# One core, attention and a routed mixture of experts: weights loaded early, late tokens in memory, two shared quads moved, scatters in pairs, first rows in four loads

## What is computed

```python
x = x + tanh(g_xattn[0]) * attention(layernorm(x), ctx, ctx, masks, Wq, bq, Wk, bk, Wv, bv, Wo, bo)
h = layernorm(x)
probs = softmax(h @ router_w + router_b)
topk_p, topk_i = top_k(probs, 2);  topk_p /= sum(topk_p)
for e in range(8):
    moe += combine[e] * (gelu((h @ w1[e] + b1[e]) * gate[e]) @ w2[e] + b2[e])
shared = (gelu((h @ sw1 + sb1) * sgate) @ sw2 + sb2) * sigmoid(shared_weight)
x = x + tanh(g_ffn[0]) * layernorm(moe + shared) * (ln_g, ln_b)
```

## Time and profile before

| | |
|---|---|
| median of 3 runs | 815.27 us (813.66 to 815.3) |
| the profiled execution | 814.22 us, span 812.4 us |
| mean granted clock of PE | 0.95 |
| busy, share of the span | PE 87%, PEld 67%, DVE 76%, ACT 65%, POOL 34% |
| stages by the span | attention to 439.8, experts to 723.5, combine to the end |

### The profile page before, as it was taken

One profiled execution on the slowest core, in us unless ns is written; L12 is line 12 of the kernel. 1 busy time (PEld: TensorE's weight loads), 2 busy tenths in 40 slices (PEclk: granted clock), 3 DMA queues, 4 the chain that ended last, 5 costly groups with the idle time before them and its releaser, 6 DMA issues. The chain is left out here.

```text
span 812.4 us, 25014 instructions
## 1 busy us (share of the span) xinstructions
PE 703.1 (87%) x8074; PEld 546.8 (67%) x8075; DVE 619.3 (76%) x2328; ACT 526.3 (65%) x1117; POOL 274.6 (34%) x293
## 2 busy tenths in 40 slices
PE   2799999999999999999953799999999998967930
PEld 1466666666666666666631599999999997945620
DVE  5788988888888888888764577766666664629998
ACT  2678877878778787777520565666555664528873
POOL 5000033222333223233345146655555554520000
PEclk9999999999999999999955999999999999989975
DMA  4111121222321232311113822222222222244552
GB/s 126 40 41 48 54 81 44 70 65 76 84 81 51 61 88 73 83 42 38 38 47 132 207 67 78 75 78 68 74 69 75 73 70 62 68 114 135 171 145 87
DMA packets 74961, 64.59 MB, mean 80 GB/s; under 512 B 8320, under 2 KB 62848, under 8 KB 74624
## 3 DMA queue, kind: packets, MB, share of 16 engines
q1 hardware_dynamic: 53360, 32.96, 16.1%
q0 software_dynamic: 8448, 17.45, 6.6%
q10 hardware_dynamic: 13072, 13.12, 5.1%
HBM read 36.22 MB, written 23.09 MB: 73 GB/s over the span
## 5 line engine op out<-in xcount | busy, mean ns | idle before, releaser
L181 POOL DMA_INDIRECT expert_lists<-xn,slots x128 | 124.5, 973 | 311.9 <-PE pair L421 194.6
L1257 ACT ACTIVATE hT<-pair,b1g_c,gate_c 128x256 f32<-128x256 f32 x272 | 138.4, 562 | 101.5 <-PE pair L79 94.8
L1382 POOL DMA_INDIRECT expert_results<-y,dest x136 | 138.9, 1022 | 130.6 <-DVE y L1359 81.3
L1196 PE MATMUL pair<-w,hT 128*128 x1088 | 134.7, 277 | 0.0
L1196 PEld LDWEIGHTS pair<-w,hT 128*128 128x128 f32 x1088 | 127.0, 192 | 2.1 <-issue 0.5
L898 ACT ACTIVATE PT<-pair 128x512 f32<-128x512 f32 x128 | 75.5, 591 | 45.0 <-PE pair L434 45.0
L77 PE MATMUL pair<-rT,w_now 128*128 128x256 f32 x276 | 83.8, 303 | 4.6 <-ACT hT L1257 3.8
L577 DVE TENSOR_REDUCE mx<-pair 128x16 f32<-128x1024 f32 x64 | 78.2, 1223 | 10.0 <-PE pair L404 8.5
L1330 DVE CAST w_now<-w 128x1024 fp32r x71 | 52.7, 742 | 36.3 <-issue 36.3
L79 PE MATMUL pair<-rT,w_now 128*128 128x256 f32 x276 | 78.5, 284 | 0.0
L78 PE MATMUL pair<-rT,w_now 128*128 128x256 f32 x276 | 78.4, 284 | 0.0
(11 more groups left out here) (182 smaller groups left out, 1422.8 us busy)
## 6 DMA issues: line engine op xcount, KB each, us to landing
rows<-expert_lists SPq DMA_DIRECT2D x70, 130.0 KB
yin<-expert_results SPq DMA_DIRECT2D x16, 512.0 KB, 5.3
x_all<-in_x SPq DMA_DIRECT2D x16, 256.0 KB, 4.5
cT<-in_ctx_T SPq DMA_DIRECT2D x16, 256.0 KB
pad_k<-in_mask_BxS_ik SPq DMA_DIRECT2D x16, 256.0 KB
xn2T<-x2T ACTq DMA_DIRECT2D x16, 256.0 KB
w<-in_w ACTq DMA_DIRECT2D x4, 1024.0 KB, 15.2
out<-res ACTq DMA_DIRECT2D x7, 512.0 KB, 4.6
```

The source lines that it names most:

```text
L181: po.indirect_dma_start(lists[:, :], bass.IndirectOffsetOnAxis(ap=m.slots[:, par, t, k:k + 1], axis=0), m.xn2[:, par, t, :], None).then_in ...
L1196: last = pe.matmul(y_ps[par][:, h * D:(h + 1) * D], hT[:, par, c, h * P:(h + 1) * P], w2[:, bass.ds(e, 1), c, :].rearrange("p a d -> p (a ...
L1257: ac.activation(hT[:, par, c, :], h_ps[par][c // 2][:, (c % 2) * SL:(c % 2 + 1) * SL], ACT.Gelu, bias=b1g_c[:, c, bass.ds(e, 1)], scale=ga ...
L1382: po.indirect_dma_start(results[:, :], bass.IndirectOffsetOnAxis(ap=dest[:, par, h, :], axis=0), y[:, par, h, :], None).then_inc(sent[par] ...
```

## The change

`DRAINED = 2` quads of the shared expert go into attention's drain. Their hidden layer stands on PE behind the transposed logits of quad 14, their gelu on ACT behind the DMA of quad 15 (into `prob`), their second layer on PE ahead of the prefix sums of quad 15, and their copies at ACT's end of the block. `prepare` moves from (NQ, 1) to (NQ - 1, 1). `w2` and the first half of `w1` are loaded in attention, 256 KB with each of the last 12 quads' loads on SP. `x2T` of quads 4 to 15 goes to memory (`late_tokens`) and comes back in 12 loads of 256 KB, issued by ACT in the first 16 tiles of experts, which are now written out on ACT too. In combine the first group's rows come in four loads of 256 KB, and ACT weighs them ahead of its first gelus. Scatters are two a tile step, at all four steps; slots are ready before the weights' part of `route_b`.

```diff
     m.xn2T = sb("xn2T", [P, EARLY * QW])
+    m.w2 = sb("w2", [P, E, F // P, D])
+    m.w1a = sb("w1a", [P, E // 2, F])
...
+            def early_weights(i):
+                if i < E:
+                    sp.dma_start(m.w2[:, i], a["w2"][:, i]).then_inc(m.weights_in, 16)
+                else:
+                    sp.dma_start(m.w1a[:, i - E], a["w1"][:, i - E]).then_inc(m.weights_in, 16)
             for q in range(2, NQ):
                 load_x(q, q % 2)
                 load(q, q % 2)
                 later_load(q - 4)
+                if q >= NQ - 12:
+                    early_weights(q - (NQ - 12))
...
@@ PE, attention
+            def early_hidden(q):
+                need(pe, exped, NT - 1)
+                need(pe, max_flat, NT - 1)
+                pe.wait_ge(m.prepared, 6)
+                pe.wait_ge(x2T_kept[q], 16)
+                for c in range(SC):
+                    pe.matmul(banks[2 * q + c][:, :], m.sw1[:, c * P:(c + 1) * P], xn2T[:, q * QW:(q + 1) * QW],
+                              start=True, stop=True).then_inc(sh_done, 1)
...
                     feed_a(u, par, q)
+                    if (q, u) == (NQ, 3):
+                        for i in range(DRAINED):
+                            early_hidden(i)
+                    if (q, u) == (NQ + 1, 3):
+                        for i in range(DRAINED):
+                            early_second(i)
@@ DVE, attention
-                    if (q, u) == (NQ, 1):
+                    if (q, u) == (NQ - 1, 1):
                         prepare()
@@ ACT, attention
+                    if (q, u) == (NQ + 1, 3):
+                        need(ac, turned, NT - 1, per=2)
+                        for i in range(DRAINED):
+                            for c in range(SC):
+                                ac.wait_ge(sh_done, i * SC + c + 1)
+                                ac.activation(prob[:, i, c * QW:(c + 1) * QW], banks[2 * i + c][:, :], ACT.Gelu,
...
-                        ac.dma_start(xn2T[:, cols_of((q - 2) * QT, QT)], x2T[:, par, :]).then_inc(x2T_kept[par], 16)
+                        kept = (xn2T[:, cols_of((q - 2) * QT, QT)] if q - 2 < EARLY else
+                                tokens[:, (q - 2 - EARLY) * QW:(q - 1 - EARLY) * QW])
+                        ac.dma_start(kept, x2T[:, par, :]).then_inc(x2T_kept[par], 16)
...
+            for q in range(DRAINED):
+                ac.wait_ge(sy_done, q + 1)
+                ac.activation(xn2T[:, q * QW:(q + 1) * QW], pt_ps[q][:, :], ACT.Copy)
@@ POOL, attention
+            def scatter(n, q, first):
+                need(po, rb_step, q, per=RB_STEPS, k=3, total=NQ)
+                if q < NQ - 3:
+                    need(po, masked, n)
+                    scatter_rows(po, lists, m, q, (first,))
                     need(po, turned, n - 1, per=2)
+                    scatter_rows(po, lists, m, q, (first + 1,))
+                else:
+                    if q == NQ - 3:
+                        need(po, *((lg_done, q + 1), (lgT_done, q + 1), (pref_done, q + 1),
+                                   (xn2_ready, q + 2, QT))[first // 2], total=NQ)
+                    else:
+                        need(po, (x2T_done, lg_done, lgT_done, pref_done)[first // 2], q + 1, total=NQ)
+                    scatter_rows(po, lists, m, q, (first, first + 1))
...
+                    if u >= 2 and exists(q - 3, NQ - 1):
+                        scatter(n, q - 3, 2 * u - 4)
+                    if u < 2 and exists(q - 4, NQ - 1):
+                        scatter(n, q - 4, 2 * u + 4)
@@ ACT, experts
-            halves = [slice(k * E // 2, (k + 1) * E // 2) for k in range(2)]
-            for k, es in enumerate(halves):
-                ac.dma_start(w1[:, es, 1, :], a["w1"][:, es]).then_inc(w1_in[k], 16)
+            ac.dma_start(w1[:, E // 2:, 1, :], a["w1"][:, E // 2:]).then_inc(w1_in, 16)
             pads(ac, range(E // 2, E))
-            for es in halves:
-                ac.dma_start(w2[:, es], a["w2"][:, es]).then_inc(w2_in, 16)
...
-            iterations(ac, body)
+                if isinstance(t, int):
+                    late = NQ - EARLY
+                    for q in range(t * late // HEAD, (t + 1) * late // HEAD):
+                        ac.dma_start(m.late_T[:, q * QW:(q + 1) * QW], tokens[:, q * QW:(q + 1) * QW]).then_inc(m.late_in, 16)
+            iterations(ac, body, HEAD // 2)
@@ combine
-            for g in range(NGR):
+            for i in range(2):
+                for k in range(2):
+                    at = i * H * P + k * TOK
+                    sp.dma_start(yin[:, 0, k, i * H:(i + 1) * H], results[at:at + H * P, :]
+                                 .rearrange("(t p) d -> p t d", p=P)).then_inc(first_in[i][k], 16)
+            for g in range(1, NGR):
                 load(g)
...
+            weigh(0)
             gelu(EARLY)
             gelu(EARLY + 1)
-            weigh(0)
             weigh(1)
```

123 lines of the change are left out of this document (66 added, 57 removed).

## The result

The changed kernel takes 825.12 us (median of 4 runs, 821.45 to 826.34), the kernel before 814.75 beside it: a ratio of 1.0112 (95% interval 1.0094 to 1.0131). It is **1.1% slower**; 808.5 was forecast, and faster. The profiled execution took 821.45 us with a span of 819.6, against 814.22 and 812.4.

A forecast was written before the change was run, and what follows sets the result against it. PE was taken to bound attention and experts, so edits pay only in attention's drain and the starts of experts and combine. -6.6 - 0.8 + 1.25 = -6.15 gives 808.1 on 814.22, set at 808.5; range 803.5 to 813.0.

The forecast's parts named there:

- At nothing: Attention's steady part and experts' loop: weight loads, late tokens' stores and loads, and moved scatters would cost no time.
- 12 weight loads at nothing: Attention: weight loads behind each quad's own loads on SP take 1 to 2 us of some 20 available, costing nothing.
- (a): Attention's drain: prepare leaves tile 63's residual and takes DVE time in quad 15; cost 0.6 us, between 0 and 2.2.
- (b): Attention's drain: hidden-layer matmuls on PE delay quad 15's transposes by 0.7 us, between 0 and 1.8.
- second rival: Attention's drain, warm: PE keeps full clock from the first two quads, no release is late; 804.7 us, chance 0.17.
- (c): Attention's drain: second layers ahead of quad 15's prefix sums delay these by 4.7 us, between 3.2 and 6.3.
- (d): End of attention's drain: quad 14's last two scatters wait for the prefix sums and delay the start of experts 0.9 us.
- (e): Attention's drain: late release of quad 15's logits, 5.05 us, goes; that of its prefix sums, 1.9, stays: -5.05 us.
- The likeliest rival: Attention's drain: late releases return; 813.1 us with both, 811.2 with the logits' alone; chance 0.22.
- Start of experts: With most weights loaded earlier, scatters land sooner and DVE's 6.61 us wait goes: -6.6 us, or -5 if later.
- Combine: Start of combine: half the rows arrive earlier, so the add starts sooner: -0.8 us, between -0.3 and -1.25.
- Token loads: Experts' first tiles: 12 late-token loads cost nothing; the rival had them stretch tiles, 817.7 us at 0.8 each, chance 0.06.

The follow-up runs named there:

- waits_swapped: The changed kernel with two wait lines of the scatters exchanged, masked now ahead of rb_step; 1.0044 of the kernel before.
- before_again: The kernel before, unchanged, run once on chip C as reference for traces; 24.21 us a quad, no ratio.
- the fixed ones: Three changed kernels with old scatter pace, late second layers, weighing behind gelus, earlier drain scatters; 0.9975, 0.9987 and 0.9959 of the kernel before.
- weights_late: The changed kernel with w2 and the first half of w1 loaded at the start of experts again; 1.0124 of the kernel before.
- order_old: The changed kernel with the old order of route_b's steps only; 1.0054 of the kernel before.
- changed_weigh_late: The changed kernel with ACT's weigh(0) behind the two gelus of combine again; 1.0124 of the kernel before.
- fixed_all_again: Chip A repeat: changed kernel with old scatter pace, late second layers, weighing behind gelus, earlier drain scatters; 0.9987 of the kernel before.

## Why the prediction was wrong, step by step

- **"At nothing ... The moved scatters are far ahead of the reuse of their rows in the steady part"** is the step that failed. I costed the scatters by what they wait for and by who needs their rows, and not by the moment at which POOL issues them. The reordering of waits wasn't costed at all. In place of nothing the runs show 0.56 us a quad, 5.6 us between tiles 16 and 56: with `masked` as the separate wait the scatters start 0.5 us later and hold casts on DVE and matmuls on PE. Exchanging the two lines takes 8.6 us off T63. None of the four rivals had it, and the one that ended slower had another mechanism.
- *The whole*: 821.45 against 808.1 is 13.4 us, of which 8.3 lie ahead of T63, 1.4 in the drain, 1.7 at the start of experts, 1.6 in its loop and 0.4 in combine. The failed step is the largest part, not all: with the waits exchanged the kernel is still not faster than before (1.0044), and with the second layers late as well it is level (0.9994).
- *12 weight loads at nothing*: right (23.72 a quad with and without them). The stores of late tokens were never tried alone; with loads and pairs they cost nothing in the steady quads (24.21 in waits_swapped and in before_again).
- *(a) prepare, 0.6*: right in size; between tiles 61 and 62 the changed kernel loses 1.1, the fixed ones 0.75.
- *(b) +0.7 for the hidden layers*: mis-sized, and of the wrong sign. I took half clock in part (5.70); they took 3.67, and prefix sums, transposes and logits behind them ran at full clock (1.00 between 424 and 432 us, where the kernel before had 0.50 between 417 and 431). Without its late release, T63 to LT was 25.5 before; it is 21.6 now: 3.8 us less, where I had 0.1 more. The warm drain of the second rival is here in its first half; the second layers, at 0.57, are not.
- *(c) +4.7*: right, the prefix sums at `LT` + 9.2 instead of + 8.75; both second layers took 6.09 where I had 5.45.
- *(d) +0.9 for quad 14's last two scatters*: failed. POOL wasn't free: at `LT` + 11.8 it had just ended ten others, its pair then waited for the late release of the prefix sums, and B came 3.6 us behind DVE's last work (447.21). Before, B stood 1.6 us behind the start of the positions, now 5.3: 3.7 us instead of 0.9.
- *(e) "I take the 5.05 as gone and the 1.9 as staying"*: the 5.05 moved. The release of the prefix sums is 4.1 us late instead of 1.9, and POOL's run now ends there. The likeliest rival (late releases back) was right that they return, wrong on where. That the drain came out at +2.0 behind T63, near my +0.65, is luck: (b) was 3.9 us better than I had it, (c) 0.5, (d) 2.8 and (e) 2.0 worse.
- *Start of experts, -6.6*: -4.9. Eight scatters over at B + 11.5, as forecast, but SP's first rows at B + 15.9 instead of at most 14.5, and PE's first tile at half clock. weights_late shows the term itself: 5 us. That the weights and not POOL's queue made the scatters land late is borne out (SP's wait fell from 15.2 to 8.9; on chip B it is 9.7 in order_old and 16.1 in weights_late); but my argument for it, 9.7 us as longer than POOL's whole run at its pitch, was wrong, since that run takes 9.8.
- *Combine, -0.8*: -0.4 in this pair of profiles, about 0 over all of them. The reason that I had named against it (gelus behind the weighing) is likely, not shown: changed_weigh_late took as long as changed_again.
- *Token loads*: 1.6 us over the whole loop, 0.13 a load if all of it is theirs, which no run tried alone. The rival of 0.8 a load is out.
- *Range*: its lower end, the warm drain with (b) at its best, comes to 804.0 by the terms given, not 803.5. It decided nothing.
- *ACT_TABLE_LOAD*: 1.28 us, with the gelu 0.02 behind it (432.20, 433.50); the row held, and the 2.66 of the Trainium skill ("ScalarE: Activation LUTs", "What ACT_TABLE_LOAD costs") did not show.
- *Not forecast*: 1.3 us at the start-up. In all profiles of the changed family on chips A and C but one (fixed_all_again), tile 8 stands 1.4 to 3.2 us behind that of the unchanged kernels; why isn't known.

## What to carry to other kernels

A wait that is long met is not free if it makes an instruction's waits two: ask which of them is issued by itself, and put the one that ends last where it stays on the instruction, or wait for the old one once, ahead. When GpSimd's work is moved, look at which short VectorE operation and which matmul on a critical chain now falls beside it, tile by tile; busy shares don't show it. An operation can be held and cost nothing (the cast of tile 0 on chips A and C): compare the pitch of each tile before you name a culprit. And long runs of indirect DMAs beside a chain of short dependent steps cost the chain its releases, on all chips here but B: spread them, and measure the chain with the scatters taken away before you price what stands in it.
